# Attention, edge stage and aggregations on one core: the last key block as a full 128-row block with zero padding instead of a 20-row block

## The chip, the cores and the metric

The kernel runs on one core of a Trainium2 chip. The metric is the device time of one execution in microseconds (us); lower is better. The core has five engines that run their own instruction streams and meet only at semaphores: TensorE (PE, with its weight loads shown apart as PEld), VectorE (DVE), ScalarE (ACT), GpSimd (POOL) and SyncE (SP), which here only issues DMAs.

## What is computed

Four graph layers over N = 2708 nodes with D = 512 features. Each layer's output is added to its input and layer-normalised.

```
x = layernorm(x + attention(x, adj))              # layer 0: 8 heads, masked softmax over all keys
x = layernorm(x + relu((adj @ x) @ W1.T + b1))    # layer 1
x = layernorm(x + edge(x, adj))                   # layer 2: softmax of h @ h.T masked by adj, times node weights
x = layernorm(x + relu(norm_adj @ x @ W3.T + b3)) # layer 3
```

In layer 0 every query row takes a softmax over 2708 keys and multiplies it with the 2708 value rows; layers 1 to 3 multiply a 2708-wide row of (weighted) adjacency with 2708 rows of features. All these products contract over the 2708 nodes.

## The kernel before

The 2708 nodes are cut into T = 22 blocks of P = 128 rows; the last one has LAST = 20 real rows, and NP = 2816 is the padded count. Data are split into a high and a low float16 half, so that each product is made of two or three float16 products, (high, high), (high, low), (low, high).

Layer 0 (`attention`) loops over 22 tiles of 128 queries and, in each, over 8 heads: 176 units. A unit's work on PE is: scores against all keys in three pieces (L667), ten 128-column transposes of the exponentiated scores of the last ten key blocks (`turn`, L678), and the product of 22 key blocks with the values into `ps_pv` (`products`, L687): three matmuls for each block, of 65, 64 and 65 columns. The first TK = 12 blocks ("far") are turned by DMA transposes that SP issues (L587), the last ten ("near") by PE. The units are pipelined: in step h PE makes the scores of unit h, the transposes of unit h-2 and the products of unit h-3. The order in a step of PE is written out by hand: scores 0 and 1, turn group 0, far products, turn groups 1 and 2, scores 2, near products. In steps 5 and 6 the finished tile before is projected by `wo` as well; in step 6 that is 12 matmuls of 512 columns ahead of everything else.

The other engines follow in step: DVE masks each piece of scores (L803) and makes the low half of the near blocks (L822), ACT takes the exponentials and the high halves, POOL makes the low half of the far blocks (L622) and, in step 6, the layer norm of the tile before (L421 to L433), whose DMA store SP issues between two transposes. PE waits for DVE before each piece of scores (`slot_free`), for ACT before a turn, for the DMA transposes before the far products (`far_ready`).

The tile loop is unrolled by two from tile 3 on (`pairs`), so PE's program jumps back after every second tile.

Layer 2's `edge_attention` works on 22 tiles of 128 rows: scores for the tile (three pieces, some turned from earlier rows), softmax, DMA transposes, and `products` of the tile before: 22 blocks times three matmuls of 512 columns (L1082). Layers 1 and 3 end in `aggregate`: 22 tiles, 22 blocks times two matmuls of 512 columns in one accumulation (L1337).

In all of these the last block is cut to its real rows by

```
def rows_of(k):
    return P if k < T - 1 else LAST
```

so that the operands of block 21 are slices of 20 partitions. In the profile such matmuls have the shape `20*128` (20 contracted rows times 128 stationary columns). The transposes of block 21 take a slice of 20 columns and have the shape `128*20`.

Of the kernel before, what the change touches and what calls it, by code (L numbers as in the profile page):

```python
# [23 lines left out]
P = 128  # L24
N = 2708
# [3 lines left out]
T = -(-N // P)  # L29
NP = T * P  # L30
LAST = N - (T - 1) * P
# [20 lines left out]
def wait_apart(eng, sem, value, met):  # L52


    if not isinstance(value, int):
        value = eng.to_reg(value)
    eng.wait_ge(met, 1)  # L57
    eng.wait_ge(sem, value)  # L58


def rows_of(k):
    return P if k < T - 1 else LAST


class Scope:
# [383 lines left out]
TURN_GROUPS = [list(range(k, min(k + GB, T))) for k in range(TK, T, GB)]  # L449
NT = len(TURN_GROUPS)  # L450
# [9 lines left out]
def attention(nc, layer, x_rows, out_rows, q_rows, adj_rows, kk, vv, wo, ident):  # L460
# [5 lines left out]
    with ExitStack() as ctx:  # L466
        s = Scope(nc, ctx, "att", layer)
# [1 line left out]
        off_diag = s.sb("off_diag", [P, P])  # L469
        xres = s.sb("xres", [P, D])  # L470
        q = s.sb("q", [P, 2, 2, 2, J, P], F16)
        sc = s.sb("scores", [P, 2, N])
        part = [s.sb(f"part_{a}", [P, 2, TK * P], F16) for a in ("high", "low")]
        far = [s.sb(f"far_{a}", [P, 2, TK, P], F16) for a in ("high", "low")]
        near = [s.sb(f"near_{a}", [P, 2, T - TK, P], F16) for a in ("high", "low")]
# [7 lines left out]
        ps_t = s.ps("ps_t", [P, NT, BANK])  # L483
        ps_pv = s.ps("ps_pv", [P, BANK])
# [4 lines left out]
        pad_clear, ones_ready = s.sem("pad_clear"), s.sem("ones_ready")  # L489
# [8 lines left out]
        part_low = [s.sem(f"part_low{c}") for c in range(len(FAR))]  # L498
        far_ready = [s.sem(f"far_ready{v}") for v in range(2)]
        far_used = s.sem("far_used")  # L500
        rest_clear = s.sem("rest_clear")
        turned = s.sem("turned")
        near_high = [s.sem(f"near_high{g}") for g in range(NT)]
        near_low = [s.sem(f"near_low{g}") for g in range(NT)]
# [92 lines left out]
        @block.gpsimd  # L597
        def _(pool):
            nc.gpsimd.memset(adj[:, :, N:NP], -BIG).then_inc(pad_clear, 1)
            nc.gpsimd.memset(vv[:, :, :, P:P + 1], 1.0).then_inc(ones_ready, 1)  # L600
            norm.exponent(nc, pool)
            nc.gpsimd.tensor_scalar(out=off_diag[:, :], in0=ident[:, :], scalar1=-1.0, scalar2=1.0, op0=ALU.mult,
                                    op1=ALU.add).then_inc(off_diag_ready, 1)

            def bias(m, u, n):
                lo, width = ADJ_PARTS[n]
                wait_apart(pool, adj_loaded[n][u], 16 * m + 16, pad_clear)
                nc.gpsimd.tensor_scalar(out=adj[:, u, lo:lo + width], in0=adj[:, u, lo:lo + width], scalar1=BIG,
                                        scalar2=-BIG, op0=ALU.mult, op1=ALU.add).then_inc(bias_ready, 1)

            def diagonal(m, u):

                t = 2 * m + u
                wait_apart(pool, bias_ready, len(ADJ_PARTS) * (t + 1), pad_clear)
                part_of = adj[:, u, bass.ds(t * P, P)]
                nc.gpsimd.tensor_tensor(out=part_of, in0=part_of, in1=off_diag[:, :], op=ALU.mult) \
                    .then_inc(diag_ready, 1)

            def low(i, v, c):
                lo, width = FAR[c]  # L620
                wait_apart(pool, part_high[c], i + 1, pad_clear)
                nc.gpsimd.tensor_tensor(out=part[1][:, v, lo:lo + width], in0=sc[:, v, lo:lo + width],  # L622
                                        in1=part[0][:, v, lo:lo + width], op=ALU.subtract).then_inc(part_low[c], 1)

            def step(m, u, h, on):
                if on(1):
                    i, _t, _u, h1, same = unit(m, u, h, 1)
                    v = h1 % 2
                    lo, width = FAR[0]
                    if not early(i, 2):  # L630
                        wait_apart(pool, far_ready[v], 32 * same, pad_clear)
                    wait_apart(pool, exp_done, NC * i + 1, pad_clear)
                    nc.gpsimd.tensor_copy(part[0][:, v, lo:lo + width], sc[:, v, lo:lo + width]) \  # L633
                        .then_inc(part_high[0], 1)
                for n, bias_h in enumerate(BIAS_STEPS):
                    if h == bias_h and not is_tile(m, u, T - 1) and not is_tile(m, u, T):
                        bias(*after(m, u), n)
                if h == 4 and not is_tile(m, u, 0):
                    pool.wait_ge(rinv_ready, 2 * m + u)
                    nc.gpsimd.tensor_tensor(out=o[:, :].rearrange("p (h k) -> p h k", h=H), in0=pv[:, 1 - u, :, 0:KD],  # L640
                                            in1=rinv[:, :, :].broadcast_to([P, H, KD]), op=ALU.mult) \
                        .then_inc(o_done, 1)
                if h == 6 and not is_tile(m, u, 0):
                    norm.finish(nc, pool, *before(m, u))
                if on(1):
                    low(i, v, 0)
                    low(i, v, 1)
                if h == BIAS_STEPS[-1] and not is_tile(m, u, T - 1) and not is_tile(m, u, T):
                    diagonal(*after(m, u))

            for n in range(len(ADJ_PARTS)):
                bias(0, 0, n)
            pool.wait_ge(off_diag_ready, 1)
            diagonal(0, 0)
            all_steps(pool, step)

        @block.tensor
        def _(pe):
# [12 lines left out]
            def turn(i, v, g):  # L671
                if g == 0:
                    pe.wait_ge(exp_done, NC * (i + 1))
                if not early(i, 1):
                    pe.wait_ge(near_low[g], i)
                for n, k in enumerate(TURN_GROUPS[g]):
                    r = rows_of(k)
                    mm = nc.tensor.transpose(ps_t[0:r, g, n * P:(n + 1) * P], sc[:, v, k * P:k * P + r], ident[:, :])  # L678
                mm.then_inc(turned, 1)

            def products(v, h, keys):
                for k in keys:
                    r = rows_of(k)
                    halves, n = (far, k) if k < TK else (near, k - TK)
                    for a, b in ((0, 0), (0, 1), (1, 0)):
                        cols = slice(KD, P + 1) if b == 0 else slice(0, KD)
                        mm = nc.tensor.matmul(ps_pv[:, 0:cols.stop - cols.start], halves[a][0:r, v, n, :],  # L687
                                              vv[0:r, k, h, cols], start=k == 0 and a + b == 0,
                                              stop=k == T - 1 and a == 1)
                return mm  # L690

# [43 lines left out]
                if on(3):  # L735
                    near_products(k, h3 % 2, h3)

            pe.wait_ge(ones_ready, 1)
            pe.wait_ge(rest_clear, 1)
            all_steps(pe, step)  # L740

        @block.scalar
# [51 lines left out]
        def _(dve):  # L794
# [68 lines left out]
                if on(2):  # L863
                    near_rest(j, h2 % 2, 1)

            rest = len(TURN_GROUPS[-1]) * P
            nc.vector.memset(ps_t[:, NT - 1, rest - P:rest], 0.0).then_inc(rest_clear, 1)
            dve.wait_ge(pad_clear, 1)
            all_steps(dve, step)

# [1 line left out]
def edge_attention(nc, layer, x_rows, out_rows, scores_rows, adj_rows, adj, ht, sup, z, bias_row, degree, ident):  # L872
# [3 lines left out]
    with ExitStack() as ctx:  # L876
        s = Scope(nc, ctx, "edge", layer)
        bias = s.sb("bias", [P, N])
        xres = s.sb("xres", [P, 2, D])
        sc = s.sb("scores", [P, 2, N])  # L880
        part = [s.sb(f"part_{a}", [P, NP], F16) for a in ("high", "low")]
        pt = [s.sb(f"pt_{a}", [P, T, P], F16) for a in ("high", "low")]
# [11 lines left out]
        ps_o = s.ps("ps_o", [P, 2, BANK])  # L894
# [150 lines left out]
        def _(pe):  # L1045
# [27 lines left out]
            def products(m, u):  # L1073
                t = 2 * m + u
                for c in range(NC):
                    pe.wait_ge(pt_turned[c], 32 * (t + 1))
                    if c == 0 and not (isinstance(m, int) and m == 0):
                        pe.wait_ge(r_ready, t - 1)
                    for k in range(*keys_of(c).indices(T)):
                        r = rows_of(k)  # L1080
                        for a, b in ((0, 0), (0, 1), (1, 0)):
                            mm = nc.tensor.matmul(ps_o[:, u, :], pt[a][0:r, k, :], sup[b][0:r, k, :],  # L1082
                                                  start=k == 0 and a + b == 0, stop=k == T - 1 and a == 1)
                    mm.then_inc(used, 1)

# [179 lines left out]
def aggregate(nc, layer, tag, x_rows, out_rows, adj_cols, a32, y, bias_row, ident, dcol=None):  # L1265
# [5 lines left out]
    with ExitStack() as ctx:  # L1271
        s = Scope(nc, ctx, tag, layer)
        a16 = s.sb("adj16", [P, 2, T, P], F16)
# [3 lines left out]
        ps = s.ps("ps", [P, 2, BANK])  # L1277
# [49 lines left out]
        @block.tensor  # L1327
        def _(pe):
            def step(m, u):
                t = 2 * m + u  # L1330
                pe.wait_ge(narrowed if dcol is None else diag_ready, t + 1)
                if not (isinstance(m, int) and m == 0):
                    pe.wait_ge(biased, t - 1)
                for k in range(T):
                    r = rows_of(k)
                    for b in range(2):
                        mm = nc.tensor.matmul(ps[:, u, :], a16[0:r, u, k, :], y[b][0:r, k, :],  # L1337
                                              start=k == 0 and b == 0, stop=k == T - 1 and b == 1)
                mm.then_inc(summed, 1)

            step(0, 0)
            step(0, 1)
            pairs(pe, 2, T, step)
# [165 lines left out]
```

## Time and profile before

| what | value |
|---|---|
| time, median of 3 runs | 2666.68 us (2665.36 to 2668.89) |
| span of the profiled execution, first to last instruction | 2664.4 us |
| PE busy | 2511.2 us (94%) |
| PE weight loads busy | 1583.2 us (59%) |
| DVE busy | 1549.8 us (58%) |
| ACT busy | 1364.3 us (51%) |
| POOL busy | 1134.1 us (43%) |
| mean granted TensorE clock | 0.972 of full |

Busy times of PE count a matmul from its start to its modelled end, and matmuls overlap, so a PE that is busy all the time says little of its pace; the distance from one matmul's start to the next one's start tells that. No time but the span is given for the profiled execution itself; it lies 2.3 us under the median of the runs.

### The profile page before, as it was taken

The numbers are of one execution on the slowest core, as the hardware profiler recorded it, in microseconds if no ns is written. First come the engines' busy times: TensorE is split into PE (matmuls) and PEld (weight loads), VectorE is DVE, ScalarE is ACT, GpSimd is POOL, SyncE is SP. The second block draws the span as 40 slices with busy tenths as digits, with TensorE's granted clock in tenths as the row PEclk, the third lists the DMA queues.
The fourth block names the chain that finished last, engine by engine and source line by source line (L and its number), as shares of the span: only waits on it lengthen the run. The fifth ranks groups of instructions, "written<-read, shape, count | busy, mean of one in ns | idle before, by whom it ended". The sixth has DMA issues, their size and how long they took to land. (4 is left out here: it accounts for less than half of the span.)

```text
span 2664.4 us, 67769 instructions
## 1 busy us (share of the span) xinstructions
PE 2511.2 (94%) x25068; PEld 1583.2 (59%) x25068; DVE 1549.8 (58%) x3014; ACT 1364.3 (51%) x2024; POOL 1134.1 (43%) x967
## 2 busy tenths in 40 slices
PE   7997999999999999999969998999999999979998
PEld 6885776767777777777734443774444444434443
DVE  3346887878878788778832222554545556633222
ACT  3336887877878778778823221323424334423221
POOL 0006887878778778778800222001111111110222
PEclk9998999999999999999989999999999999989999
DMA  3117999999999899999843564314556668543554
GB/s 131 63 56 154 188 179 162 189 168 172 174 167 176 161 177 177 162 172 186 150 125 101 203 207 147 107 36 129 153 164 164 178 178 219 145 136 100 203 201 142
DMA packets 777899, 412.88 MB, mean 155 GB/s; under 512 B 690656, under 2 KB 711904, under 8 KB 769248
## 3 DMA queue, kind: packets, MB, share of 16 engines
q1 hardware_dynamic: 777696, 409.82, 66.4%
q8 instruction: 171, 2.80, 0.4%
q14 instruction: 32, 0.26, 0.0%
HBM read 201.15 MB, written 38.44 MB: 90 GB/s over the span
## 5 line engine op out<-in xcount | busy, mean ns | idle before, releaser
L803 DVE CUSTOM_DVE_ANT_0 att_scores<-att_slots,att_adj 128x1024 f32<-128x1024 f32 x528 | 576.1, 1091 | 75.4 <-PE att_slots L667 33.7
L622 POOL TENSOR_TENSOR att_part_low<-att_scores,att_part_high 128x1024 f16<-128x1024 f32 x352 | 575.4, 1651 | 73.0 <-ACT att_part_high L787 61.7
L748 ACT ACTIVATE att_scores<-att_scores,att_nmax 128x1024 f32<-128x1024 f32 x528 | 551.9, 1046 | 23.5 <-DVE att_lifted L814 19.5
L667 PE MATMUL att_slots<-l_kk,att_q 128*128 128x512 f16 x2112 | 478.2, 363 | 48.8 <-issue 34.7
L1337 PE MATMUL a_ps<-l_y,a_adj 128*128 128x512 f16 (+1 forms) x1936 | 429.9, 381 | 9.0 <-DVE a_adj L1351 4.7
L757 ACT ACTIVATE att_near_high<-att_ps_t 128x512 f16<-128x512 f32 x528 | 258.5, 524 | 223.8 <-PE att_ps_t L678 220.4
L822 DVE TENSOR_TENSOR att_near_low<-att_ps_t,att_near_high 128x512 f16<-128x512 f32 x528 | 316.4, 599 | 66.1 <-ACT att_near_high L757 65.6
L1337 PEld LDWEIGHTS a_ps<-l_y,a_adj 128*128 128x128 f16 (+1 forms) x1936 | 182.6, 98 | 256.3 <-issue 40.2
L667 PEld LDWEIGHTS att_slots<-l_kk,att_q 128*128 128x128 f16 x2112 | 199.0, 100 | 213.2 <-issue 54.1
L1082 PE MATMUL edge_ps_o<-l_sup,edge_pt_high 128*128 128x512 f16 x968 | 288.1, 379 | 0.0
L1321 ACT ACTIVATE a_adj<-l_adj 128x2816 f16<-128x2816 f32 x44 | 112.0, 2550 | 298.4 <-DMA l_adj<-in_adj_cols 278.4
L678 PE MATMUL att_ps_t<-all_ident,att_scores 128*128 128x128 f32 x1760 | 259.9, 279 | 2.1 <-ACT att_scores L748 2.1
L633 POOL CAST att_part_high<-att_scores 128x1024 f16<-128x1024 f32 x176 | 182.8, 1038 | 102.6 <-ACT att_scores L748 101.9
L687 PE MATMUL att_ps_pv<-l_vv,att_far_high 128*128 128x65 f16 (+1 forms) x4224 | 220.3, 194 | 3.0 <-DMA att_far_low<-att_part_low 3.0
L687 PEld LDWEIGHTS att_ps_pv<-l_vv,att_far_high 128*128 128x128 f16 x4224 | 215.3, 98 | 5.8 <-issue 3.5
L1068 PE MATMUL edge_slots<-l_ht 128*128 128x512 f16 x1104 | 203.4, 345 | 16.1 <-DVE edge_mx L1176 14.4
L687 PE MATMUL att_ps_pv<-l_vv,att_far_low 128*128 128x65 f16 x2112 | 214.6, 195 | 0.0
L678 PEld LDWEIGHTS att_ps_t<-all_ident,att_scores 128*128 128x128 f32 x1760 | 189.4, 138 | 32.6 <-issue 10.8
L687 PEld LDWEIGHTS att_ps_pv<-l_vv,att_near_high 128*128 128x128 f16 x3520 | 182.2, 97 | 42.5 <-issue 0.2
L1023 POOL TENSOR_TENSOR edge_xb<-edge_xres,all_b_row 128x512 f32<-128x512 f32 x22 | 27.9, 1270 | 415.1 <-DVE edge_residual L1220 407.3
L687 PE MATMUL att_ps_pv<-l_vv,att_near_high 128*128 128x65 f16 x3520 | 201.8, 192 | 0.0
L687 PEld LDWEIGHTS att_ps_pv<-l_vv,att_far_low 128*128 128x128 f16 x2112 | 196.1, 98 | 0.0
(149 smaller groups left out, 3865.0 us busy)
## 6 DMA issues: line engine op xcount, KB each, us to landing
l_adj<-in_adj_cols SPq DMA_DIRECT2D x44, 1408.0 KB, 6.2
l_adj_tiles<-in_adj SPq DMA_DIRECT2D x22, 1354.0 KB, 6.0
att_adj<-in_adj SPq DMA_DIRECT2D x66, 384.0 KB, 4.3
p_x_in<-x SPq DMA_DIRECT2D x66, 256.0 KB, 2.6
att_q<-q_rows SPq DMA_DIRECT2D x44, 256.0 KB, 3.8
a_xres<-x SPq DMA_DIRECT2D x44, 256.0 KB, 2.8
scores_rows<-edge_raw SPq DMA_DIRECT2D x8, 842.0 KB, 3.5
p_x_in<-in_x SPq DMA_DIRECT2D x22, 256.0 KB, 2.7
```

Of the source, the lines that this page charges most:

```text
L622: nc.gpsimd.tensor_tensor(out=part[1][:, v, lo:lo + width], in0=sc[:, v, lo:lo + width], in1=part[0][:, v, lo:lo + width], op=ALU.subtract ...
L633: nc.gpsimd.tensor_copy(part[0][:, v, lo:lo + width], sc[:, v, lo:lo + width]) \
L667: mm = nc.tensor.matmul(slots[:, slot, z:z + w], q[:, u, h % 2, a, h // 2, :], kk[:, h, lo + z:lo + z + w], start=a == 0, stop=a == 1)
L678: mm = nc.tensor.transpose(ps_t[0:r, g, n * P:(n + 1) * P], sc[:, v, k * P:k * P + r], ident[:, :])
L687: mm = nc.tensor.matmul(ps_pv[:, 0:cols.stop - cols.start], halves[a][0:r, v, n, :], vv[0:r, k, h, cols], start=k == 0 and a + b == 0, sto ...
L748: nc.scalar.activation(sc[:, v, lo:lo + width], sc[:, v, lo:lo + width], ACT.Exp, bias=nmax[:, v:v + 1], scale=-1.0).then_inc(exp_done, 1)
L757: nc.scalar.activation(near[0][:, v, n:n + len(tiles), :], ps_t[:, g, 0:w].rearrange("p (k r) -> p k r", r=P), ACT.Copy) \
L803: nc.vector.tensor_tensor_reduce(out=sc[:, v, lo:lo + width], in0=slots[:, (NC * h + c) % 2, 0:width], in1=adj[:, u, lo:lo + width], scale ...
L822: nc.vector.tensor_tensor(out=near[1][:, v, n:n + len(tiles), :], in0=ps_t[:, g, 0:w].rearrange("p (k r) -> p k r", r=P), in1=near[0][:, v ...
L1068: mm = nc.tensor.matmul(slots[:, slot, z:z + w], ht[a][:, j, bass.ds(t * P, P)], ht[b][:, j, lo + z:lo + z + w], start=k == 0, stop=k == l ...
L1082: mm = nc.tensor.matmul(ps_o[:, u, :], pt[a][0:r, k, :], sup[b][0:r, k, :], start=k == 0 and a + b == 0, stop=k == T - 1 and a == 1)
L1337: mm = nc.tensor.matmul(ps[:, u, :], a16[0:r, u, k, :], y[b][0:r, k, :], start=k == 0 and b == 0, stop=k == T - 1 and b == 1)
```

## The change

`rows_of` goes away: every block is contracted over 128 rows, and what lies beyond node 2708 must be zero. The adjacency, the edge stage's halves and the projected rows are padded with zeros already. In attention the scores tile grows from N to NP columns, and POOL clears its 108 extra columns once for both buffers; the column of ones behind the values, which sums the softmax's denominator, is set to zero in the padding rows of block 21. DVE's one clearing of the unused part of `ps_t` goes away, and PE waits once for POOL's new clearings.

```
-        sc = s.sb("scores", [P, 2, N])
+        sc = s.sb("scores", [P, 2, NP])
...
             nc.gpsimd.memset(adj[:, :, N:NP], -BIG).then_inc(pad_clear, 1)
-            nc.gpsimd.memset(vv[:, :, :, P:P + 1], 1.0).then_inc(ones_ready, 1)
+            nc.gpsimd.memset(sc[:, :, N:NP], 0.0).then_inc(tail_clear, 1)
+            nc.gpsimd.memset(vv[:, 0:T - 1, :, P:P + 1], 1.0).then_inc(ones_ready, 1)
+            nc.gpsimd.memset(vv[:, T - 1, :, P:P + 1], 0.0).then_inc(ones_ready, 1)
+            pool.wait_ge(ones_ready, 2)
+            nc.gpsimd.memset(vv[0:LAST, T - 1, :, P:P + 1], 1.0).then_inc(ones_ready, 1)
...
-                    r = rows_of(k)
-                    mm = nc.tensor.transpose(ps_t[0:r, g, n * P:(n + 1) * P], sc[:, v, k * P:k * P + r], ident[:, :])
+                    mm = nc.tensor.transpose(ps_t[:, g, n * P:(n + 1) * P], sc[:, v, k * P:(k + 1) * P], ident[:, :])
...
-                        mm = nc.tensor.matmul(ps_pv[:, 0:cols.stop - cols.start], halves[a][0:r, v, n, :],
-                                              vv[0:r, k, h, cols], start=k == 0 and a + b == 0,
+                        mm = nc.tensor.matmul(ps_pv[:, 0:cols.stop - cols.start], halves[a][:, v, n, :],
+                                              vv[:, k, h, cols], start=k == 0 and a + b == 0,
                                               stop=k == T - 1 and a == 1)
...
-            pe.wait_ge(ones_ready, 1)
-            pe.wait_ge(rest_clear, 1)
+            pe.wait_ge(ones_ready, 3)
+            pe.wait_ge(tail_clear, 1)
...
-            rest = len(TURN_GROUPS[-1]) * P
-            nc.vector.memset(ps_t[:, NT - 1, rest - P:rest], 0.0).then_inc(rest_clear, 1)
...
-                            mm = nc.tensor.matmul(ps_o[:, u, :], pt[a][0:r, k, :], sup[b][0:r, k, :],
+                            mm = nc.tensor.matmul(ps_o[:, u, :], pt[a][:, k, :], sup[b][:, k, :],
...
-                        mm = nc.tensor.matmul(ps[:, u, :], a16[0:r, u, k, :], y[b][0:r, k, :],
+                        mm = nc.tensor.matmul(ps[:, u, :], a16[:, u, k, :], y[b][:, k, :],
```

No instruction changes its place among the matmuls; what differs is the shape of block 21's. On PE in attention, between the far products and the third piece of scores, the program before has five full transposes and one whose output has 20 rows:

```order
604 L687 MATMUL att_ps_pv<-l_vv,att_far_low 128x65
605 L678 MATMUL att_ps_t<-all_ident,att_scores 128x128 x5
606 L678 MATMUL att_ps_t<-all_ident,att_scores 20x128
607 L667 MATMUL att_slots<-l_kk,att_q 128x512
608 L667 MATMUL att_slots<-l_kk,att_q 128x404
```

The changed program has six full ones in that place:

```order
602 L685 MATMUL att_ps_pv<-l_vv,att_far_low 128x65
603 L677 MATMUL att_ps_t<-all_ident,att_scores 128x128 x6
604 L667 MATMUL att_slots<-l_kk,att_q 128x512
605 L667 MATMUL att_slots<-l_kk,att_q 128x404
606 L667 MATMUL att_slots<-l_kk,att_q 128x512
```

The count of matmuls is the same. On POOL, at the start of attention, the program before has these rows ahead of the first work on the adjacency (L608):

```order
12 L599 MEMSET att_adj 128x2x108
13 L600 MEMSET l_vv 128x176
14 L415 MEMSET att_power 128x1
15 L602 ISA
16 L602 TENSOR_SCALAR att_off_diag<-all_ident 128x128
17 L608 TENSOR_SCALAR att_adj<-att_adj 128x768 x3
```

The changed program has three short clearings more in that place:

```order
12 L595 MEMSET att_adj 128x2x108
13 L596 MEMSET att_scores 128x2x108
14 L597 MEMSET l_vv 128x168
15 L598 MEMSET l_vv 128x8
16 L600 MEMSET l_vv 20x8
17 L411 MEMSET att_power 128x1
18 L602 ISA
19 L602 TENSOR_SCALAR att_off_diag<-all_ident 128x128
20 L608 TENSOR_SCALAR att_adj<-att_adj 128x768 x3
```

They stand once in the program, outside every loop, and what follows on POOL is the same.

## Rows read from the trace of the kernel before

**Rows 1.** Windows by stage: window, length, busy us (instructions), PEclk, DMA share, GB/s.

```profile
230.00:450.00 220.00, 219.50 (x3300) 167.25 (x3299) 192.70 (x428) 184.91 (x300) 189.67 (x152) 1.00 1.03 185
...
1834.00:2190.00 356.00, 356.00 (x1778) 167.07 (x1776) 183.58 (x278) 130.69 (x174) 57.29 (x56) 1.00 0.62 166
...
2440.00:2655.00 215.00, 214.90 (x968) 91.30 (x968) 54.89 (x106) 53.17 (x21) 59.69 (x63) 0.99 0.54 184
```

**Rows 2.** Timeline, PE, attention: start us, length us, engine, line, operation, count.

```profile
512.98 1.69 PE L667 MATMUL att_slots<-l_kk,att_q 128*128 128x512 f16 x8
...
518.60 1.69 PE L667 MATMUL att_slots<-l_kk,att_q 128*128 128x512 f16 x8
```

**Rows 3.** Group of weight loads, PEld: count, busy us, mean ns of one, idle before.

```profile
L1337 PEld LDWEIGHTS a_ps<-l_y,a_adj 128*128 128x128 f16 (+1 forms) x1936 | 182.6, 98 | 256.3 <-issue 40.2
```

**Rows 4.** Timeline, end of one unit's products in attention (PE's own rows).

```profile
1007.77 0.22 PE L687 MATMUL att_ps_pv<-l_vv,att_near_high 128*128 128x65 f16 x2
...
1007.86 0.22 PE L687 MATMUL att_ps_pv<-l_vv,att_near_high 128*128 128x65 f16 x2
...
1007.92 0.19 PE L687 MATMUL att_ps_pv<-l_vv,att_near_low 128*128 128x65 f16 x1
...
1008.05 0.23 PE L687 MATMUL att_ps_pv<-l_vv,att_near_high 20*128 20x65 f16 x2
...
1008.24 0.39 PE L98 MATMUL att_ps_t<-l_wo_high,att_ot 128*128 128x512 f16 x1
```

**Rows 5.** Timeline, PE: six transposes, the sixth of 20 columns, and the scores behind.

```profile
516.04 0.85 PE L678 MATMUL att_ps_t<-all_ident,att_scores 128*128 128x128 f32 x6
516.72 0.94 PE L667 MATMUL att_slots<-l_kk,att_q 128*128 128x512 f16 x4
```

**Rows 6.** Timeline, PE, aggregation: inside one tile, then across one tile's end.

```profile
1468.69 4.48 PE L1337 MATMUL a_ps<-l_y,a_adj 128*128 128x512 f16 x20
...
1471.71 9.65 PE L1337 MATMUL a_ps<-l_y,a_adj 128*128 128x512 f16 x43
```

**Rows 7.** Timeline, PE, edge stage: end of a tile's products; then scores that waited.

```profile
2016.28 0.38 PE L1082 MATMUL edge_ps_o<-l_sup,edge_pt_low 128*128 128x512 f16 x1
2016.59 0.60 PE L1082 MATMUL edge_ps_o<-l_sup,edge_pt_high 20*128 20x512 f16 x2
...
2017.34 0.33 PE L1060 MATMUL edge_slots<-all_ident,edge_mirror 128*128 128x128 f32 x1
...
2276.35 3.53 PE L1068 MATMUL edge_slots<-l_ht 128*128 128x512 f16 x24 [1.50 <-DVE edge_mx L1176]
```

**Rows 8.** Timeline and DMA landing around a tile's end in attention.

```profile
503.85 1.23 DVE L803 CUSTOM_DVE_ANT_0 att_scores<-att_slots,att_adj 128x1024 f32<-128x1024 f32 x1 [0.63 <-POOL att_part_low L622]
...
506.81 1.10 DVE L803 CUSTOM_DVE_ANT_0 att_scores<-att_slots,att_adj 128x916 f32<-128x916 f32 x1
...
507.36 1.69 PE L667 MATMUL att_slots<-l_kk,att_q 128*128 128x512 f16 x8
...
512.88 1.81 SPq L587 DMA_TRANSPOSE att_far_high<-att_part_high  x1
...
514.95 1.62 SPq L587 DMA_TRANSPOSE att_far_low<-att_part_low  x1
...
DMA to landing us min/median/max: 5.3/5.3/5.3
...
520.56 0.22 PE L687 MATMUL att_ps_pv<-l_vv,att_far_high 128*128 128x65 f16 x2
```

**Rows 9.** Timeline and window at the jump back of attention's tile loop.

```profile
454.72 2.31 PE L667 MATMUL att_slots<-l_kk,att_q 128*128 128x512 f16 x5 [3.83 <-issue]
...
452.98:463.30 10.32, 7.79 (x56) 5.21 (x57) 2.79 (x5) 1.59 (x3) 3.16 (x2) 0.50 0.61 94
```

**Rows 10.** Timeline, POOL, its first work behind the clearings of attention.

```profile
213.59 1.80 POOL L608 TENSOR_SCALAR att_adj<-att_adj 128x768 f32<-128x768 f32 x2 [4.80 <-DMA att_adj<-in_adj]
```

**Rows 11.** Timeline, DVE, attention: idle time ahead of an instruction in a plain step.

```profile
515.77 0.69 DVE L822 TENSOR_TENSOR att_near_low<-att_ps_t,att_near_high 128x512 f16<-128x512 f32 x1 [0.37 <-ACT att_near_high L757]
```

More of the change, by code:

```diff
@@ L58, in wait_apart @@
     eng.wait_ge(sem, value)
-def rows_of(k):
-    return P if k < T - 1 else LAST
 class Scope:
@@ L500, in attention @@
         far_used = s.sem("far_used")
-        rest_clear = s.sem("rest_clear")
+        tail_clear = s.sem("tail_clear")
         turned = s.sem("turned")
@@ L682, in products @@
                 for k in keys:
-                    r = rows_of(k)
                     halves, n = (far, k) if k < TK else (near, k - TK)
@@ L1079, in products @@
                     for k in range(*keys_of(c).indices(T)):
-                        r = rows_of(k)
                         for a, b in ((0, 0), (0, 1), (1, 0)):
-                            mm = nc.tensor.matmul(ps_o[:, u, :], pt[a][0:r, k, :], sup[b][0:r, k, :],
+                            mm = nc.tensor.matmul(ps_o[:, u, :], pt[a][:, k, :], sup[b][:, k, :],
                                                   start=k == 0 and a + b == 0, stop=k == T - 1 and a == 1)
@@ L1334, in step @@
                 for k in range(T):
-                    r = rows_of(k)
                     for b in range(2):
-                        mm = nc.tensor.matmul(ps[:, u, :], a16[0:r, u, k, :], y[b][0:r, k, :],
+                        mm = nc.tensor.matmul(ps[:, u, :], a16[:, u, k, :], y[b][:, k, :],
                                               start=k == 0 and b == 0, stop=k == T - 1 and b == 1)
```

## The prediction

> **What bounds the kernel now.** I read the trace by stage first, then PE's timeline, then who waits for whom. Three stages hold nearly all matmuls of block 21: attention, the edge stage's products and the two aggregations. In each of them PE is busy throughout its plain stretch: 219.50 of 220 us, 356 of 356 and 214.90 of 215, at a granted clock of 1.00 or 0.99 [rows 1]. DVE is next in attention with 192.70 of 220. Busy alone proves little, since matmuls overlap. The pace shows it: the scores of two consecutive plain steps of attention start at 512.98 and 518.60, 5.62 us apart [rows 2], and PE's busy time leaves no idle time inside such a step, while DVE idles 0.37 us at the head of its step [rows 11]. So attention goes at PE's pace, and a microsecond taken from PE's stream there is one taken from the kernel, until another engine or the DMA queue is caught up with. The DMA queue is the candidate: its share is 1.03 in attention, against 0.62 and 0.54 in the other two stages [rows 1].
>
> **What the 20-row block costs.** At the end of a unit's products, full-row blocks of three matmuls start 0.09 us apart (1007.77, 1007.86). Then the last full-row matmul starts at 1007.92, the first 20-row one at 1008.05, and the matmul behind the block at 1008.24 [rows 4]. Fewer rows make nothing shorter; on the contrary PE starts nothing new for about 0.1 us both when it enters the block and when it leaves it. With full rows I expect one start after 0.03 us and the block's 0.09 us, so 0.12 instead of 0.32: **0.20 us a unit**. Over 176 units that is 35.2 us.
>
> In the aggregations 20 starts inside a tile span 4.48 us. Less one matmul's own 0.38 us [rows 7], 19 distances take 4.10 us, 0.2158 each. Across a tile's end 43 starts take 9.65, so 42 distances take 9.27 us, where 42 times 0.2158 is 9.06: **0.21 us a tile** [rows 6]. Two layers of 22 tiles give 9.2 us.
>
> In the edge stage the last full-row start is at 2016.28 and the first matmul behind the block at 2017.34: 1.06 us for four distances, against 0.86 at 0.2158, **0.20 us a tile** [rows 7]. In the last band of tiles, though, PE waits for DVE at scores 2 (tiles 16 to 21; one such wait is 1.50 us, [rows 7]). DVE's chain there begins where the products end, so the entry into the block is saved, but not the empty time behind its last matmul (0.09 us), which the wait covers anyway: 0.11 for six tiles, 0.20 for sixteen, together 3.9 us.
>
> The sum of what can be saved is 35.2 + 9.2 + 3.9 = 48.3 us.
>
> **What the other parts cost.** The transposes: six, the last of them with 20 columns, start at 516.04, and the scores behind them at 516.72, so 0.113 us each with no gap at the odd one [rows 5]. A full sixth transpose is bounded by one such distance on either side; it takes the same slot, and I put the change at nothing. Here the Trainium skill, page "TensorEngine Tiling (Array Packing)", section "Key Properties", says that a change of the tiling mode drains the engine, and it lists modes narrow in columns as well as in rows. By it the 20-column transposes should pay as the 20-row products do, and padding them would save about another 35 us (an estimate: 176 times the product's 0.20). The rows show a drain for the rows only, so the sum goes by the rows.
>
> The three added clearings on POOL run once and are narrow (216, 8 and 8 elements a partition). Behind them POOL idles 4.80 us for the adjacency's DMA [rows 10]; that wait hides them. Were the cover gone, they would cost less than those 4.80 us. DVE's removed clearing lay under the same load. The wider scores tile changes no operation's width outside the transposes.
>
> **What is given back in attention.** With 5.42 us a step PE comes closer to its suppliers. DVE had 0.37 us idle a step and keeps some 0.17. The tight place is a tile's end. POOL's layer norm holds up the low halves, DVE waits 0.63 us for them, and then its mask of scores 2 ends at 507.91 (506.81 + 1.10). PE's scores 1 that need that buffer start four matmuls after 507.36, at 508.22: 0.31 us to spare [rows 8]. The norm hangs on the projection two steps before, so PE arrives 0.40 us earlier relative to it and waits 0.1. Two steps later the far products of head 7 start at 520.56, and their last transpose, issued at 514.95, lands 5.3 us later at 520.25: again 0.31 us to spare [rows 8]. PE has four shortened block ends between the projection and there, 0.80 us. If the transposes move with PE, nothing is lost; if their landing is set by the busy queue alone, PE waits 0.80 - 0.1 - 0.31 = 0.4. I take 0.3, nearer to the queue, because of the share of 1.03. Behind PE's scores 2 and near products stand the next step's scores, so such a wait delays all engines equally.
>
> Of 21 tile ends, 8 are jumps back of the loop, where PE idles 3.83 us for nothing that the profile shows [rows 9] and DMA and DVE run ahead; they lose nothing. The other 13 give back 0.4 each, **5.2 us**. The first three steps and the last one, where PE already waits for DMA or runs out of units, give back 0.20 each, 0.8 us.
>
> 48.3 - 5.2 - 0.8 = 42.3. From the profiled span of 2664.4 that is 2622.1; the median of the runs lies 2.3 us over the span, so the forecast is **2624.4 us**.
>
> **Rivals.** *The DMA queue takes over attention.* If transposes and adjacency loads already fill the queue, a part of attention's gain returns as waits on `far_ready`. For it: the share of 1.03 and 0.31 us to spare. Against it: PE never waits for the queue in the plain stretch. Half of the gain lost is 17.6 instead of the 6.0 us counted above, 2636; all of it lost leaves 13.1 us, 2654.
>
> *Only the entry is saved.* If the empty time behind the block belongs to the end of an accumulation and not to its rows, a half stays: about 0.1 of 0.2 everywhere, and little given back, so 24 us, 2643. Against it: matmuls of the projection end an accumulation too, and nothing in the profile shows such a gap there.
>
> *Slower: the clock.* At the loop's jump PE's idle time of 3.83 us is followed by 10.3 us at a granted 0.50, the 1.2 GHz level [rows 9]. If the new wait at each of the 13 other tile ends brought the clock down in the same way, each could cost half of up to 10.3 us besides the wait, 5 us, 65 in all: 2664.4 - 48.3 + 65 + 2.3 = 2683. It decides from about 3.7 us a tile end (48.3 / 13). Against it: the wait that I expect is 0.4 us and not 3.8.
>
> *Full-row loads become visible.* A weight load takes 98 ns [rows 3]. There are 3 x 176 + 2 x 44 + 3 x 22 = 682 in block 21; if none were hidden they would cost 67 us and the time would be 2685. But matmuls of full-row blocks already start 0.2158 and 0.03 us apart, so their loads do run beside other matmuls. The Trainium skill, page "TensorE: Matmul & The Clock Gate", section "Part 3: Packing small matmuls", says that a load overlaps a running matmul only if their row groups differ, which would give this rival; the trace disagrees in every full-row block.
>
> *Nothing changes*, if block 21's empty time only moves to another wait: 2666.7.
>
> **How the numbers follow.** The forecast case (2617 to 2632 by itself: from 0 to twice the 6 us given back, and some 2 us for where the clock's low stretches fall) gets 0.70. The queue's case gets 0.17, most of it below 2645. Only the entry gets 0.06. No measurable change gets 0.03, the clock 0.03, visible loads 0.01. The range has to leave out at most 2 in 10: its low end is the whole 48.3 + 0.5 us with luck at the clock, 2615, its high end the two partial cases, **2615 to 2644**. A measurement of this kernel tells about 0.2% from no change, 5.3 us, so faster needs a time under 2661: 0.70 + 0.17 + 0.06 = 0.93, with the queue's worst case still inside. Same gets 0.03 and slower 0.04.
>
> **What would show it.** In the changed kernel no `20*128` shape is left; the products' last block starts at the pace of the ones before, and the next matmul 0.03 us (attention) or 0.216 us (aggregation) behind it. A plain step of attention takes 5.42 us, a tile of an aggregation 9.50 us. If waits of PE on `att_far_low` or on DVE's masks of more than 1 us a tile appear, or stretches of 0.50 clock at more than 8 places in attention's loop, the forecast is wrong; if gaps of 0.1 us stay at the block's end, the drain was not of the rows.

## The result, and the profile after

The changed kernel takes 2624.21 us (median of four runs, 2622.72 to 2630.29), against 2667.78 of the kernel before beside it (four runs, 2665.36 to 2668.95): 0.9847 of the time [0.9832, 0.9863], 43.6 us less. A second set of runs, described below, gave 0.9859 [0.9843, 0.9876], 37.9 us less. The profiled execution of the changed kernel happens to be the slowest of the four: its span is 2628.5 us and its own time 2630.29. The mean granted clock is 0.971, as before (0.972).

PE in attention, timeline of the changed kernel: the scores of four consecutive steps, the first of them at a tile's end.

```profile
1206.34 1.90 PE L667 MATMUL att_slots<-l_kk,att_q 128*128 128x512 f16 x8
...
1211.98 1.68 PE L667 MATMUL att_slots<-l_kk,att_q 128*128 128x512 f16 x8
...
1217.40 1.67 PE L667 MATMUL att_slots<-l_kk,att_q 128*128 128x512 f16 x8
...
1222.84 1.67 PE L667 MATMUL att_slots<-l_kk,att_q 128*128 128x512 f16 x8
```

From 1211.98 to 1217.40 a plain step takes 5.42 us, where it took 5.62 [rows 2]. The first row also shows a small new wait: its eight matmuls take 1.90 us and not 1.67, and its step 5.64.

The end of a unit's products, which stood apart in [rows 4]:

```profile
483.14 0.19 PE L685 MATMUL att_ps_pv<-l_vv,att_near_low 128*128 128x65 f16 x1
483.18 0.22 PE L685 MATMUL att_ps_pv<-l_vv,att_near_high 128*128 128x65 f16 x2
483.23 0.20 PE L685 MATMUL att_ps_pv<-l_vv,att_near_low 128*128 128x65 f16 x1
483.27 0.63 PE L709 MATMUL att_ps_t<-all_ident,att_o 128*128 128x128 f32 x4
```

The last block's first matmul starts 0.04 us after the one ahead of it (0.13 before), and what comes behind the block starts 0.04 us after its last one. Both empty times of 0.1 us are gone.

The six transposes, all of 128 columns now, and the scores behind them:

```profile
991.09 0.85 PE L677 MATMUL att_ps_t<-all_ident,att_scores 128*128 128x128 f32 x6
991.77 0.94 PE L667 MATMUL att_slots<-l_kk,att_q 128*128 128x512 f16 x4
```

0.68 us from the first transpose to the scores, exactly as in [rows 5].

The aggregations: 48 starts, so across at least one tile's end, and then all of layer 3's.

```profile
1440.74 10.52 PE L1331 MATMUL a_ps<-l_y,a_adj 128*128 128x512 f16 x48
...
2408.38 210.79 PE L1331 MATMUL a_ps<-l_y,a_adj 128*128 128x512 f16 x968 [4.74 <-DVE a_adj L1345]
```

Less one matmul's 0.38 us, 47 distances take 10.14 us, 0.2157 each. That is the pace inside a tile of before [rows 6], and the tile's end is no longer to be seen. The same layer took 214.96 us before (2440.10 to 2655.06 in the timeline of before).

The end of a tile's products in the edge stage, which answers to [rows 7]:

```profile
2011.11 0.59 PE L1077 MATMUL edge_ps_o<-l_sup,edge_pt_high 128*128 128x512 f16 x2
2011.54 0.38 PE L1077 MATMUL edge_ps_o<-l_sup,edge_pt_low 128*128 128x512 f16 x1
2011.76 1.04 PE L1056 MATMUL edge_slots<-all_ident,edge_mirror 128*128 128x128 f32 x8
```

The block's last start and the next matmul are 0.22 us apart, the plain pace.

I cut both traces at the same matmuls, from a stage's first start to its last end in PE's timeline (us; the second profile of the changed kernel comes from the second set of runs):

| stage | before | changed | changed, second profile | forecast of the difference |
|---|---|---|---|---|
| attention | 1127.63 | 1101.98 | 1097.94 | -29.2 |
| aggregation, layer 1 | 214.90 | 210.55 | 210.55 | -4.6 |
| edge stage | 551.40 | 547.38 | 547.41 | -3.9 |
| aggregation, layer 3 | 214.96 | 210.79 | 210.79 | -4.6 |
| all the rest | 555.5 | 557.8 | 557.8 | 0 |

The aggregations give 8.5 us, the edge stage 4.0. Attention gives 25.7 in the one profile and 29.7 in the other. The rest of the kernel, which the change hardly touches, was 2.3 us longer in both profiles; the six partly changed kernels below have 555.2 to 557.7 us there, so this is within the spread between executions.

What PE waits for, in the whole changed kernel (us in total, times, longest):

```profile
PE att_slots L667 <- issue: 38.0, 16, 3.9
...
PE att_slots L667 <- DVE att_least L801: 6.4, 6, 4.6
PE att_ps_pv L685 <- DMA att_far_low<-att_part_low: 5.5, 9, 2.5
```

Before, the same three rows say 34.7, 4.8 and 3.0 us. So attention has new waits, of a few us in all.

### The profile page after: what moved, and what is told of

Same layout as the page of the kernel before. It is cut to its first block and busy times, and to the rows that moved or that the text cites. A ratio compares the mean times of both kernels' runs of the same rounds, so it can differ in the third digit from the quotient of the medians.

```text
span 2628.5 us, 67771 instructions
## 1 busy us (share of the span) xinstructions
PE 2465.8 (94%) x25068; PEld 1577.6 (60%) x25068; DVE 1545.4 (59%) x3013; ACT 1359.4 (52%) x2024; POOL 1134.0 (43%) x970
## 5 line engine op out<-in xcount | busy, mean ns | idle before, releaser
L1331 PE MATMUL a_ps<-l_y,a_adj 128*128 128x512 f16 x1936 | 421.3, 381 | 9.0 <-DVE a_adj L1345 4.7
L1331 PEld LDWEIGHTS a_ps<-l_y,a_adj 128*128 128x128 f16 x1936 | 190.0, 98 | 240.3 <-DVE a_adj L1345 5.2
L685 PEld LDWEIGHTS att_ps_pv<-l_vv,att_far_high 128*128 128x128 f16 x4224 | 214.0, 98 | 11.5 <-issue 7.2
L677 PEld LDWEIGHTS att_ps_t<-all_ident,att_scores 128*128 128x128 f32 x1760 | 198.6, 143 | 35.3 <-issue 13.2
L685 PE MATMUL att_ps_pv<-l_vv,att_near_high 128*128 128x65 f16 x3520 | 183.5, 192 | 0.0
```

The lines of the kernel that those rows point to most:

```text
L677: mm = nc.tensor.transpose(ps_t[:, g, n * P:(n + 1) * P], sc[:, v, k * P:(k + 1) * P], ident[:, :])
L1331: mm = nc.tensor.matmul(ps[:, u, :], a16[:, u, k, :], y[b][:, k, :], start=k == 0 and b == 0, stop=k == T - 1 and b == 1)
```

## The experiments

**The parts apart.** The first kernel keeps the full rows in attention alone:

```
-  matmul(ps_o[:, u, :], pt[a][:, k, :], sup[b][:, k, :], ...)
+  matmul(ps_o[:, u, :], pt[a][0:rows_of(k), k, :], sup[b][0:rows_of(k), k, :], ...)
...
-  matmul(ps[:, u, :], a16[:, u, k, :], y[b][:, k, :], ...)
+  matmul(ps[:, u, :], a16[0:rows_of(k), u, k, :], y[b][0:rows_of(k), k, :], ...)
```

> The changed kernel with block 21 cut to 20 rows again in the edge stage and the aggregations; only attention keeps full rows. Theory (PE empties for 0.1 us on entering and on leaving a block of fewer rows): the edge stage and the two aggregations go back to the length they had before (551.4, 214.9 and 215.0 us), attention stays some 30 us shorter, in all about 31 us under before, near 2637. Rival (the DMA queue eats most of attention's gain and the total came from elsewhere): under 15 us gained.

Measured: 2640.13 us, 0.9898 [0.9881, 0.9914], 26.4 us less than before. Attention takes 1106.61 us, the aggregations 214.90 and 214.96, the edge stage 551.29, as before the change.

The second is the kernel before with the full rows in the edge stage and the aggregations alone (the same two lines the other way round).

> The kernel before with full rows in the edge stage and the aggregations alone. Theory: 4.0 us in the edge stage and 8.6 us in the two aggregations, about 12.6 us under before, near 2655; together with the attention-only kernel's gain it makes up that of the whole change. Rival (the stages' savings overlap or shift the clock's low stretches): the two gains do not add up to within 4 us.

Measured: 2650.43 us, 0.9935 [0.9918, 0.9952], 16.1 us less. Attention takes 1123.70, the aggregations 210.79 and 211.97, the edge stage 548.40. The two parts add up: 26.4 + 16.1 = 42.5 us, where the whole change gave 43.6 and 37.9. The 16.1 us are 3.5 more than expected. By its three stages the second part is worth 10.1 us; attention, which its edit doesn't touch, was 3.9 us shorter in this profile than in that of before, and such a spread between executions has to be kept in mind for all that follows.

**Do the transposes pay for 20 columns?** The changed kernel with the transposes of block 21 narrow again, and DVE's clearing back:

```
+  r = rows_of(k)
-  transpose(ps_t[:, g, n * P:(n + 1) * P], sc[:, v, k * P:(k + 1) * P], ident[:, :])
+  transpose(ps_t[0:r, g, n * P:(n + 1) * P], sc[:, v, k * P:k * P + r], ident[:, :])
```

> The changed kernel, but the transposes of block 21 take 20 columns again and DVE clears the part of ps_t once as before; all products keep full rows. Theory (only a change in contracted rows empties PE): the same time as the changed kernel within 0.3%, and six transposes still take 0.68 us up to the next start. Rival (a change of tiling mode in columns drains as well): up to 35 us slower than the changed kernel.

Measured: 2625.58 us, 0.9845 [0.9829, 0.9861]: the changed kernel's time. Its group of narrow transposes, and one place in its PE timeline:

```profile
L683 PE MATMUL att_ps_t<-all_ident,att_scores 128*20 128x128 f32 x176 | 48.6, 276 | 0.0
```

```profile
487.51 0.85 PE L683 MATMUL att_ps_t<-all_ident,att_scores 128*128 128x128 f32 x6
...
488.19 0.38 PE L672 MATMUL att_slots<-l_kk,att_q 128*128 128x512 f16 x1
```

The 176 narrow transposes are there (the timeline names the group by its first), and the scores still follow 0.68 us after the first of six. A transpose of 20 columns leaves PE no empty time here; a product contracted over 20 rows does.

**How many rows are enough?** Block 21 holds zeros beyond its 20th row in the changed kernel, so it may be contracted over any number from 20 on. Two kernels take three numbers each: 32 in attention, 64 in the edge stage, 96 in the aggregations; then 97, 96 and 65.

```
-  matmul(..., halves[a][:, v, n, :], vv[:, k, h, cols], ...)
+  matmul(..., halves[a][0:(P if k < T - 1 else 32), v, n, :], vv[0:(P if k < T - 1 else 32), k, h, cols], ...)
...                                            (the other stages and numbers likewise)
```

> The changed kernel with block 21 contracted over 32 rows in attention, 64 in the edge stage and 96 in the aggregations, the added rows being zeros. If any count under 128 empties PE, all three stages are as long as before (attention 1127.6, edge 551.4, aggregations 214.9 us). If only counts that fit into a quarter or a half of the array do, which I expect, attention and the edge stage are as long as before and each aggregation takes 210.6 us. If it goes by the share of rows that is missing, the gap shrinks from 0.20 us in attention towards a quarter of it in the aggregations.

> The changed kernel with block 21 contracted over 97 rows in attention, 96 in the edge stage and 65 in the aggregations, the added rows being zeros. After 64 rows paid and 96 did not: if more than half of the array's rows is what counts, no stage has a gap and all are as long as in the changed kernel (attention about 1102, edge 547.4, aggregations 210.6 us). If the count has to be a multiple of 32 or reach 96, the aggregations with 65 rows go back to 214.9 us.

Measured, one run each: 2659.82 and 2630.01 us. The first kernel's PE timeline, at the block's end in attention, in the edge stage, and over 99 starts of an aggregation:

```profile
508.99 0.23 PE L685 MATMUL att_ps_pv<-l_vv,att_near_high 32*128 32x65 f16 x2
509.07 0.19 PE L685 MATMUL att_ps_pv<-l_vv,att_near_low 32*128 32x65 f16 x1
509.19 1.69 PE L667 MATMUL att_slots<-l_kk,att_q 128*128 128x512 f16 x8
...
2014.37 0.60 PE L1077 MATMUL edge_ps_o<-l_sup,edge_pt_high 64*128 64x512 f16 x2
2014.81 0.38 PE L1077 MATMUL edge_ps_o<-l_sup,edge_pt_low 64*128 64x512 f16 x1
2015.12 1.09 PE L1056 MATMUL edge_slots<-all_ident,edge_mirror 128*128 128x128 f32 x8
...
1468.82 21.54 PE L1331 MATMUL a_ps<-l_y,a_adj 128*128 128x512 f16 x99
```

The second kernel, in attention and over 61 starts of an aggregation:

```profile
487.70 0.22 PE L685 MATMUL att_ps_pv<-l_vv,att_near_high 97*128 97x65 f16 x2
487.76 0.19 PE L685 MATMUL att_ps_pv<-l_vv,att_near_low 97*128 97x65 f16 x1
487.79 0.38 PE L94 MATMUL att_ps_t<-l_wo_high,att_ot 128*128 128x512 f16 x1
...
1468.84 13.34 PE L1331 MATMUL a_ps<-l_y,a_adj 128*128 128x512 f16 x61
```

With 32 rows the next matmul starts 0.12 us behind the block and attention takes 1127.53 us; with 64 rows 0.31 us instead of 0.22, and the edge stage takes 551.63: both as with 20. With 96 rows the aggregation keeps 0.2159 us a start ((21.54 - 0.38) / 98), with 65 rows 0.2160 ((13.34 - 0.38) / 60), and with 97 rows in attention the gap is 0.03 us. So for matmuls of 512 columns the boundary lies between 64 rows (edge stage) and 65 (aggregations): up to 64 the empty time is paid in full, from 65 on nothing. For attention's matmuls of 64 and 65 columns it lies somewhere between 32 and 97. The Trainium skill, page "TensorEngine Tiling (Array Packing)", section "Available Configurations", lists row tilings of 32, 64 and 128 rows; the measurement agrees, if a matmul of 65 rows counts as 128. The same page of the Trainium skill lists column tilings too, but its section "Restrictions" names a transpose of f32 input among what column tiling excludes. The transposes here take f32, so the run with 20 columns does not contradict it; the prediction was wrong to read these transposes as column tilings. What a plain matmul of few columns costs, no run here shows.

**Per block, or per change of block?** In layer 1's aggregation block 10 is cut to 20 rows too, far from block 21; in layer 3's the neighbour, block 20. What these blocks hold beyond their 20th row is left out of the sums.

```
-  matmul(ps[:, u, :], a16[:, u, k, :], y[b][:, k, :], ...)
+  r = LAST if k in ((10, T - 1) if dcol is None else (T - 2, T - 1)) else P
+  matmul(ps[:, u, :], a16[0:r, u, k, :], y[b][0:r, k, :], ...)
```

> The changed kernel with 20-row blocks put back into the aggregations only (layer 1 contracts blocks 10 and 21 over 20 rows, layer 3 blocks 20 and 21; the rows of blocks 10 and 20 beyond the 20th are left out of the sums). Theory (PE empties at each change between full rows and few rows, however many cut blocks stand together): layer 1's aggregation takes 210.6 + 2 x 22 x 0.21 = 219.7 us, layer 3's about 210.8 + 22 x 0.21 = 215.4 us. Rival (each cut block costs by itself): both about 219.8 us. Rival (only the end of an accumulation costs): both 215 us, as in the kernel before.

Measured: layer 1's aggregation takes 220.70 us and layer 3's 216.34, where the changed kernel has 210.55 and 210.79. PE's timeline, some 90 starts of the one and of the other:

```profile
1449.71 20.42 PE L1332 MATMUL a_ps<-l_y,a_adj 128*128 128x512 f16 x90
```

```profile
2429.66 20.65 PE L1332 MATMUL a_ps<-l_y,a_adj 128*128 128x512 f16 x93
```

(20.42 - 0.38) / 89 is 0.2252 us a start, (20.65 - 0.38) / 92 is 0.2203. Two cut blocks apart cost 10.15 us in 22 tiles, two side by side 5.55, one alone (the kernel before) 4.35 and 4.17. Tile by tile it is clearer: from the second tile on, a tile takes 9.91 us with two cut blocks apart, 9.70 with two side by side, 9.70 with one (the kernel before) and 9.50 with none. The totals hold some 1.4 us besides, because in each stage's first tile 12 and 13 starts lie 0.4 us apart, at a granted clock of 0.50, where the changed kernel has 7 and 8 such starts. So the price is for a change between few rows and many, not for a block, and block 10, in the middle of an accumulation, pays it as the last block does.

**Where attention's gain was given back.** The prediction put the tight place at a tile's end, where POOL's layer norm holds up the low halves. This kernel moves the norm behind them:

```
-  if h == 6 and not is_tile(m, u, 0):
-      norm.finish(nc, pool, *before(m, u))
...                                            (both low halves)
+  if h == 6 and not is_tile(m, u, 0):
+      norm.finish(nc, pool, *before(m, u))
```

> The changed kernel with POOL's layer norm in step 6 put behind the two low halves instead of ahead of them. Theory (what attention gives back at a tile's end hangs on POOL's norm, which holds up the low halves): PE's wait at scores 1 two steps later goes away, and attention is 3 to 5 us shorter than in the changed kernel, near 2620. Rival (the norm's later store and the residual's release delay the next tile by as much, or the wait is the DMA queue's): within 2 us of the changed kernel.

Beside it, on the same chip, the changed kernel was run again:

> The changed kernel itself, beside the others on one chip: 1.6% under the kernel before, and a second profile of it. In the first profile attention was 25.6 us shorter than before where 29.2 had been forecast; if that was where the clock's low stretches and the loop's jumps fell, this profile shows a different length of attention; if it is the waits in the plain steps, the same one.

Measured: 2632.14 us with the norm moved, 0.9870 [0.9854, 0.9887]; 2628.06 us for the changed kernel, 0.9859 [0.9843, 0.9876]. Attention is 4.0 us shorter in the changed kernel's second profile than in its first, with nothing in the program changed; the clock's part in that is taken up below. The moved norm brings nothing. Its waits of PE on the far halves, and those of the changed kernel's second profile:

```profile
PE att_ps_pv L685 <- DMA att_far_low<-att_part_low: 8.2, 12, 3.0
```

```profile
PE att_ps_pv L685 <- DMA att_far_low<-att_part_low: 5.1, 8, 2.5
```

The wait only moved. At the tile ends the eight scores are all back at the plain pace, but one step later PE now waits 0.28 us ahead of scores 1 in 12 tiles, and the far halves come later. My reason for this experiment, that the norm's place is what costs the time, fell.

Two kernels ask how near the DMA queue is. Both load 128 KB more per tile, at head 7; one is the changed kernel, the other the kernel before.

```
+  sp.dma_start(spare[:, :], x_rows[bass.ds(t * P, P), 0:D // 2]).then_inc(spare_loaded, 16)
```

> The changed kernel with one more DMA of 128 KB in each of attention's 22 tiles, issued behind the residual's load at head 7; nothing reads it. Theory (at the end of a tile without a jump the DMA queue now sets when the far products of heads 7 and 0 to 2 may start): the load's time, some 0.7 us at the stretch's 185 GB/s, returns as waits of PE on the transposes, 13 x 0.4 to 0.7 or 5 to 9 us longer than the changed kernel. Rival (the queue still has room, the waits are of POOL and DVE alone): within 2 us of the changed kernel.

> The kernel before with the same DMA of 128 KB a tile. Theory (before, the transposes landed 0.3 us or more ahead of PE, so a part of the load is hidden): less is lost than in the changed kernel, 1 to 5 us. Rival (the queue bounds neither or both kernels alike): the same loss as in the changed kernel.

Measured: the changed kernel with the load takes 2637.15 us, 0.9896 [0.9876, 0.9915], 9.1 more than the second set's 2628.06; the kernel before with it 2668.72, 1.0012 [1.0001, 1.0024], some 3 us more (0.3 to 6.4 by the interval). PE's waits on the far halves, in the changed kernel with the load and in the one before with it:

```profile
PE att_ps_pv L691 <- DMA att_far_low<-att_part_low: 9.7, 16, 2.9
```

```profile
PE att_ps_pv L693 <- DMA att_far_low<-att_part_low: 4.3, 4, 3.4
```

The same load costs some 9 us once PE is faster and some 3 before, though the interval leaves the factor open; PE waits 16 times against 4, where without the load it was 8 or 9 times against 3. The queue is not the bound of the changed attention, but it stands closer behind PE than before.

The last kernel moves a load that is already there, that of the residual rows, from head 7 to head 3 of the next tile, out of the tight place:

```
-  if h == 7 and not is_tile(m, u, T):
+  if h == 3 and not is_tile(m, u, 0):
```

> The changed kernel with the residual's 256 KB load moved from head 7 of a tile to head 3 of the next, away from the transposes of heads 6 and 7. Theory (the queue at the tile's end): PE's waits for the far transposes of head 7 go away, 13 x 0.1 to 0.2 or 1 to 3 us shorter than the changed kernel, visible in the trace and hardly in the time. Rival (the wait moves to heads 1 and 2, where the adjacency's loads are): no gain, and PE waits there instead.

Measured: 2628.2 us, 0.9857 [0.984, 0.9875], no gain. The row of waits in the whole kernel is the changed kernel's, too:

```profile
PE att_ps_pv L685 <- DMA att_far_low<-att_part_low: 5.5, 9, 2.5
```

Added up by head from PE's starts, the waits at head 7 fell and those at head 0 grew.

## Why the prediction was right, and where its sizes were off

**What a 20-row block costs.** Right in place and size. The empty time is not a weight load that took long. PE's weight loads around [rows 4], in the kernel before:

```profile
1007.89 0.10 PEld L687 LDWEIGHTS att_ps_pv<-l_vv,att_near_low 128*128 128x128 f16 x1
1008.04 0.11 PEld L687 LDWEIGHTS att_ps_pv<-l_vv,att_near_high 20*128 20x128 f16 x2
```

The first load of 20 rows starts at 1008.04, at the end of the empty time and just ahead of its matmul at 1008.05: loads stand still as long as matmuls do. What holds both up, no row shows.

Compared start by start, the median plain step of attention is 0.207 us shorter: 0.093 at the entry into block 21, 0.016 inside it, 0.087 at the exit, and 0.011 at the start behind that. The forecast had 0.20; over 176 units this is 36.4 us instead of 35.2. The aggregations gave 8.5 us instead of 9.2 (4.35 and 4.17 in 22 tiles, 0.19 a tile), the edge stage 4.0 instead of 3.9. The sum of what can be saved is 48.9 us against 48.3 forecast.

**The transposes at nothing.** Right. The spacing is the same with 20 and with 128 columns, and the kernel with narrow ones has the changed kernel's time. The rival reading, that the narrow transposes empty PE as well, would have made that kernel some 35 us slower than the changed one.

**The clearings at nothing.** The stretch ahead of attention's first scores is 212.72 us before and 212.26 after, so nothing of them is seen.

**What is given back in attention.** That waits come back at the tile ends was right, the sum too small: this is the term that was mis-sized. Of 36.4 us attention kept 25.7 and 29.7 in the two profiles of the changed kernel. Over six profiles of kernels with more than 64 rows in attention (the changed one twice, and those with full rows in attention alone, with narrow transposes, with 97 rows and with more cut blocks) its mean is 1101.35 us; over three with 20 or 32 rows (before, full rows outside attention alone, and 32 rows) it is 1126.3. That is 24.9 us, so 11.5 are given back and not 6.0. By the same nine profiles, cut at each tile's first scores:

| part of attention | saved by 0.207 a unit | seen, mean | given back | forecast |
|---|---|---|---|---|
| tiles 0 to 3 | 6.6 | 190.8 - 187.3 = 3.5 | 3.1 | 1.8 |
| tiles 4 to 19, in the loop | 26.5 | 824.5 - 806.1 = 18.4 | 8.1 | 4.0 |

(The forecast's 13 waits of 0.4 us are put here as three in the first part and ten in the second, with 0.6 of the 0.8 us in the first.)

*The wait for DVE's mask* at scores 1 came as forecast, and larger. DVE and PE's weight loads at the tile end whose scores head the result's first rows:

```profile
1206.25 1.10 DVE L801 CUSTOM_DVE_ANT_0 att_scores<-att_slots,att_adj 128x916 f32<-128x916 f32 x1
...
1207.41 0.44 PEld L667 LDWEIGHTS att_slots<-l_kk,att_q 128*128 128x128 f16 x4 [0.54 <-DVE att_least L801]
```

The mask ends at 1207.35, PE's load starts 0.06 us later, and the eight scores take 1.90 - 1.67 = 0.23 us longer. From the starts of all tile ends there are ten such waits of 0.14 to 0.29 us in this execution and in the second profile, 2.2 and 2.3 in all; the forecast had 13 of 0.1. In [rows 8] I took all 0.31 us as spare and did not count the hand-over of 0.06; with it 0.25 remain, and the wait comes out at 0.15.

*The far halves*: at head 7 the wait was forecast as 0.3 us. At the ends of tiles it is 0.03 to 0.16 where it occurs in the first profile, and up to 0.46 in the second; that PE, held up by the mask, arrives later fits the smaller waits. But PE waits at other heads too. Added up over all starts of far products, PE waits 9.1 us (8.7 in the second profile) against 4.0 before, and only 0.7 (1.4) of what is new lies at head 7. In the first four tiles lie 2.8 of the 5.1 us that are new, 1.4 of 4.7 in the second profile. From 230 to 440 us, the changed kernel (first row) and the kernel before (second):

```profile
PE att_ps_pv L685 <- DMA att_far_low<-att_part_low: 2.6, 7, 0.6
```

```profile
PE att_ps_pv L687 <- DMA att_far_low<-att_part_low: 0.2, 1, 0.2
```

The prediction counted three steps there in which PE waits for DMA; the transposes are late over four tiles. Where it wrote "PE never waits for the queue in the plain stretch" and a single tight head, the small waits at heads 0, 1 and 2 were missed.

*The loop's jumps*: that "they lose nothing" is not settled. PE's idle time there is 38.0 and 37.6 us against 34.7. But over the nine profiles it is 36.0 to 38.0 us (mean 36.9) with more than 64 rows and 34.7 to 36.9 (mean 35.9) with 20 or 32, so most of the difference may be spread.

*The clock*: the prediction had no term for where its low stretches fall, only 2 us in a range. Between the first scores of tiles 4 and 20 the granted clock is at 0.50, the 1.2 GHz level, for 54.6 us before, 54.6 in the first profile of the changed kernel and 44.4 in the second, always at the loop's jumps (eight, eight and seven of them). Over the nine profiles this part of attention grows by 0.3 us for each us at 0.50 (a straight-line fit, give or take 0.06). That is less than half; the stretch in [rows 9], for one, begins at 452.98, while PE is still idle up to 454.72. By the same fit full rows save 21.0 us in that part at equal clock, give or take 0.9, where 22.5 were forecast.

For the first profile three terms add up: 2.2 + 5.1 + 3.3 = 10.6 us, where 36.4 - 25.7 = 10.7 are missing. For the second they give 2.3 + 4.7 + 2.9 = 9.9, where 6.7 are missing; the 10.2 us less at 0.50 make up 3.1 of the difference by the fit. By the means of the nine profiles the mask's wait is 2.3 us, the far halves 5.0, the jumps 1.0 and the clock 2.6 (54.0 us at 0.50 against 45.5), together 10.9 of the 11.5. So the two waits alone come to 7.3 us where 6.0 were forecast, and for the jumps and the clock the sum had nothing. By part it closes less well: ahead of the loop 4.8 us are missing in the first profile, and the far halves make 2.8 of them. Whether the change itself lengthens the low stretches stays open: single profiles have 44 to 61 us with more than 64 rows, and 38 to 55 with 20 or 32.

**The total.** 48.9 saved and 11.5 given back make 37.4 us, and the second set timed 37.9. The first timed 43.6, and that the forecast of 2624.4 met 2624.21 so closely is partly luck: the second set's 2628.06 is as good a measurement, and both lie in the likeliest case's own range.

**The rivals.** *The DMA queue takes over* is the one with some truth: the waits on far halves grew from 3.0 to 5.5 us (5.1 in the second profile), and the added load shows the queue near. But by PE's starts it adds 5 us, not 17.6. *Only the entry is saved* fell: the exit is 0.04 us, and the cut block in the middle of an accumulation pays as well. *Slower by the clock* fell: the mean granted clock did not move, the new waits are under 1 us and not 3.8, and the loop's low stretches stand at its jumps, as before. *Full-row loads become visible* fell: blocks of 128 rows run at the plain pace to the end. By the Trainium skill, page "TensorE: Matmul & The Clock Gate", section "Part 3: Packing small matmuls", a load overlaps only a matmul of another row group; the aggregation's 0.2157 us a start with a 98 ns load each [rows 3] stands against it. *Nothing changes* is excluded by the interval.

## What to carry to other kernels

A short block of matmuls contracted over 64 rows or fewer, among matmuls of 128, costs PE about 0.1 us when it comes and 0.1 us when it goes, and saves nothing by its fewer rows (shown here for 20, 32 and 64 rows in blocks of two and three matmuls); contract it over 65 rows or more with zeros behind, or put all short blocks side by side so that the price is paid once. Read it from the distance between starts and not from busy time: PE was "busy" through every one of these gaps. And where an engine in a tight pipeline gets 4% faster, look at each hand-over that has less to spare than the gain adds up to between two meetings, down to a hand-over's own 0.06 us.

## What the runs showed of the hardware

- The boundary is sharp: of matmuls of 512 columns, at 0.216 us a start, those with 20 and 64 rows pay, those with 65, 96 and 128 do not. Of matmuls of 64 and 65 columns, at 0.03 us a start, those with 20 and 32 rows pay, those with 97 and 128 do not. Each of 32, 64, 65, 96 and 97 was run in one or two executions.
- An f32 transpose of 20 columns among those of 128 costs nothing extra: 0.68 us for six and the scores behind, either way.
- After the change back to 128 rows the second start is late too, 0.226 us instead of 0.215.
